# Mixer and routed feed-forward layer on one core: the place of value and gate products in a TensorE step

## The chip, the cores and the metric

One core of one Trainium2 chip runs the whole program. The metric is the device time of one launch in microseconds, the median of the runs shown. TensorE (PE) multiplies matrices and transposes, VectorE (DVE) and ScalarE (ACT) work element by element and empty the PSUM banks that TensorE fills, GpSimd (POOL) does so on SBUF alone, SyncE (SP) issues most DMAs. Each engine works through its own list of instructions in order and meets the others at semaphores.

## The reference

32 batches of 512 tokens with 512 features, all in float32. First a mixing layer with 8 heads of 64, then a feed-forward layer with routing:

```python
q = layernorm(x);  k = v = ctx                     # per batch, 8 heads of 64
ig, fg = concat(q, k, v) @ igate_w.T + b, ... @ fgate_w.T + b
log_D = tril(csum(log_sigmoid(fg)) differences) + ig
D = exp(log_D - rowmax(log_D))
C = (q @ k.T / 8 + einsum('bhvc,vmhc->bhvm', q, rpe[hops])) * D
h = (C / (max(|sum C|, exp(-max)) + 1e-6)) @ v     # then normalised per head, scaled, shifted
x = x + h
y = layernorm(x)
out = x + y @ base_w.T + base_b + 2 * sum over the top-2 experts of weight * (y @ A_e.T) @ B_e.T
```

## The kernel before

**Two stages.** The first gathers rows of `rpe` for every pair of positions and multiplies them with the queries; its products go to DRAM. It is the same before and after. The second stage works in **rounds**, one per batch and two more at the end, and each round has **12 steps**. Five batches are in flight: in a round `rn` is the batch whose inputs are loaded, `rp` the one prepared (contexts and queries transposed, gates), `ra` the one whose attention is computed, `rf` and `rg` the two whose heads are normalised and which go through the feed-forward layer, `rg` being a round further. 28 rounds have all five, three in front and four behind have fewer.

**The order is written out by hand** in the `run` function of each engine, step by step; an instruction waits in its place. The tables say what is due in which step: `C_TURN` 0, 1, 2, 3; `X_TURN` 1, 3, 4, 5; `GATES` 6; `STATS` 10; `BACK` 4, 7, 10; and for the four tiles of the feed-forward layer `TURN` 3, 6, 9, 12, `ROUTE` 4, 7, 10, 13 and `BASE` 5, 8, 11, 14, of which 12, 13, 14 are steps 0, 1, 2 of the next round (tile 3, batch `rg`).

**On TensorE**, in names of the code and lines of the profile:

- `scores(s)`: products of keys and queries with 64 rows, two heads in the two halves of the array (line 1351), and then whole-array transposes that add the stored position products (line 1359). It waits for VectorE's product `mul(s-2)`.
- `weigh(s-1)`, the value product of the step before (line 1375): 128 rows by 64 columns, two heads in two column halves. It waits for `mul(s-1)`. Every third one completes a pair of heads; ScalarE then copies it (`pair_turned`, line 835, into `attT`), TensorE turns it back (`turn_back`) and ScalarE copies and squares it (`pair_out`, lines 844 and 847) for VectorE's sums (`pair_sums`, line 1080).
- `turn_context`, `turn_queries`, `turn_back` and the turn of the feed-forward tile: four whole-array transposes each (all line 1295). Contexts 0 and 1, the queries, the gates, the gate statistics and the base products all use bank 6, so each waits until the one before is copied out.
- the route product (line 1426); `gates` (line 1326), 16 products with 128 rows and 40 columns at partitions 0 and 64; `gate_stats` (line 1336), four transposes of 40 rows.
- `base(r, t)`: the first half of the base product (line 1408), the transpose of `mix` (line 1392, waits for VectorE's line 1161), the second half (1408), and the expert product (line 1410), which waits for ScalarE's copy of the turned `mix` (line 910).

Each product or transpose is followed in its step by what takes it out of PSUM: ScalarE copies contexts (798) and queries (806), gates (899) and the feed-forward tile (914). ScalarE also computes the decays (826) and the roots for the layer norms (748 and 750), VectorE the product of scores and decay `mul(s)` (1072), the query norms (1017), the feed-forward norm (1178), the router chain (1137 to 1161), the output (1123) and the gates (1032 to 1062). On VectorE a step has the order: output, query norm, gates, feed-forward norm, sums, value means, `mul(s)`, query statistics, router, layer norm input.

## Time and profile before

| | us |
|---|---|
| median of 3 runs | 4180.52 (4179.2 to 4185.26) |
| span of the profiled execution | 3689.8 |
| TensorE, VectorE, ScalarE, GpSimd busy in it | 3238.9, 2666.8, 1768.2, 2032.8 |
| stage of the rounds, from about | 1500 to the end |
| one full round | 66.95 |

The span runs from the first to the last instruction; the runs' time also holds what lies around it. A timeline row gives start and duration in us, the engine, the line, the operation with its shape, how many instructions are merged, and in brackets how long the engine idled before and what released it. `PEld` is the load of weights, which overlaps with the products. The duration of merged products is modelled at its end; where one group begins when the other is through is seen by the start of the next.

### The profile page before, as it was taken

To read this page: it belongs to the slowest core of one execution; us is meant where nothing else is said; L and a number is where in the kernel's file an instruction comes from. 1 tells how busy PE (TensorE), PEld (TensorE's weight loads), DVE (VectorE), ACT (ScalarE), POOL (GpSimd) and SP (SyncE) were. 2 spreads that over 40 slices of the span, in tenths; PEclk is the share of its full clock that TensorE was granted. 3 is DMA by queue.
4 is the path that set the end of the run, shared out by engine and by line. 5 is a ranking of instruction groups with operands and counts; after the bars stand their busy time and mean duration, and the time that the engine had idled before them with its cause. 6 is when DMAs were issued, how large, how long until landed. Compare 5 with 4: busy or idle time off the path is not lost.

```text
span 3689.8 us, 70399 instructions
## 1 busy us (share of the span) xinstructions
PE 3238.9 (88%) x24884; PEld 1901.0 (52%) x24884; DVE 2666.8 (72%) x5497; ACT 1768.2 (48%) x4225; POOL 2032.8 (55%) x2248
## 2 busy tenths in 40 slices
PE   5777777777777777699999999999999999999997
PEld 4455555554444444355555555555555555555554
DVE  5554555555555554588988889889888898898885
ACT  2444444444444444455555555555555555555552
POOL 5777777777777776144444444444444444444443
PEclk8888888889898989799999999999999999999999
DMA  8999999999999998555555555555555555555541
GB/s 259 317 317 315 320 317 316 317 323 327 330 320 323 333 324 288 186 157 169 160 154 171 156 170 158 157 170 160 156 172 154 169 156 158 169 162 157 169 142 50
DMA packets 409681, 814.16 MB, mean 221 GB/s; under 512 B 100315, under 2 KB 204763, under 8 KB 407285
## 3 DMA queue, kind: packets, MB, share of 16 engines
q1 hardware_dynamic: 303860, 453.05, 39.9%
q0 software_dynamic: 87040, 285.28, 23.7%
q10 hardware_dynamic: 18432, 71.31, 5.1%
q8 instruction: 203, 3.33, 0.4%
q14 instruction: 146, 1.19, 0.1%
HBM read 632.67 MB, written 176.69 MB: 219 GB/s over the span
## 4 chain that ended last, share of the span: by engine, by line
PE 55%; DMA 15%; POOL 11%; DVE 10%; issue 6%; ACT 2%; SPq 0%; DVEq 0%; ACTq 0%; POOLq 0%
DMA arena<-in_L_xattn_rpe_dram,arena 14%; PE psum L1408 11%; POOL arena L683 8%; PE psum L1351 7%; PE psum L1359 7%; PE psum L1375 7%; PE psum L1268 6%; PE psum L1295 5%; PE psum L1326 3%; PE psum L1410 3%; PE psum L1284 3%; PE psum L1426 3%; POOL arena L674 3%; DVE arena L1178 1%; DVE arena L1072 1%
## 5 line engine op out<-in xcount | busy, mean ns | idle before, releaser
L1268 PE MATMUL psum<-arena 128*128 128x128 f32 x4352 | 695.9, 310 | 243.1 <-DMA arena<-in_L_xattn_rpe_dram,arena 225.2
L683 POOL DMA_INDIRECT arena<-in_L_xattn_rpe_dram,arena x768 | 728.7, 949 | 268.1 <-issue 186.1
L1268 PEld LDWEIGHTS psum<-arena 128*128 128x128 f32 x4352 | 547.2, 158 | 507.0 <-DMA arena<-in_L_xattn_rpe_dram,arena 356.6
L702 POOL TENSOR_SCALAR_AFFINE_SELECT arena<-arena 128x256 f32<-128x256 f32 x256 | 107.2, 419 | 731.3 <-ACT arena L826 628.9
L826 ACT ACTIVATE arena<-arena 128x512 f32<-128x512 f32 (+3 forms) x1024 | 503.0, 559 | 7.3 <-DMA arena<-gate_rows 6.5
L1408 PE MATMUL psum<-arena 128*128 128x512 f32 x1024 | 488.1, 604 | 0.0
L513 DVE COPY arena<-psum 128x512 f32<-128x512 f32 x384 | 263.0, 688 | 280.0 <-PE psum L1268 276.4
L522 DVE COPY arena<-psum 128x416 f32<-128x416 f32 (+15 forms) x512 | 225.1, 441 | 281.3 <-PE psum L1284 278.4
L1072 DVE TENSOR_TENSOR arena<-psum,arena 128x1024 f32<-128x1024 f32 (+1 forms) x384 | 397.5, 1041 | 37.9 <-PE psum L1359 29.0
L1284 PE MATMUL psum<-arena 64*32 64x416 f32 (+7 forms) x8192 | 372.6, 434 | 27.8 <-ACT arena L750 14.9
L674 POOL DMA_INDIRECT arena<-in_L_xattn_rpe_dram,arena x320 | 303.9, 950 | 162.5 <-issue 79.8
L1351 PE MATMUL psum<-arena 64*128 64x512 f32 (+3 forms) x2048 | 381.3, 470 | 0.0
L1359 PE MATMUL psum<-arena 128*128 128x128 f32 x2560 | 364.7, 282 | 0.0
L1375 PE MATMUL psum<-arena 128*64 128x512 f32 (+3 forms) x2048 | 359.2, 450 | 2.4 <-DVE arena L1072 2.3
L522 ACT COPY arena<-psum 128x416 f32<-128x416 f32 (+15 forms) x512 | 199.1, 389 | 331.6 <-PE psum L1284 329.0
L1359 PEld LDWEIGHTS psum<-arena 128*128 128x128 f32 x2560 | 273.6, 141 | 155.5 <-issue 140.1
L513 ACT COPY arena<-psum 128x512 f32<-128x512 f32 x384 | 224.0, 588 | 257.2 <-PE psum L1268 253.7
L1295 PE MATMUL psum<-arena 128*128 128x128 f32 x2048 | 305.4, 282 | 34.4 <-DMA arena<-in_ctx_dram 11.9
L1295 PEld LDWEIGHTS psum<-arena 128*128 128x128 f32 x2048 | 225.3, 142 | 187.5 <-issue 134.6
L1408 PEld LDWEIGHTS psum<-arena 128*128 128x128 f32 x1024 | 177.3, 193 | 160.0 <-issue 152.1
L1351 PEld LDWEIGHTS psum<-arena 64*128 64x128 f32 x2048 | 165.7, 185 | 159.9 <-issue 126.7
L748 ACT ACTIVATE arena<-arena 128x1 f32<-128x1 f32 x384 | 111.3, 290 | 276.5 <-DVE arena L977 149.2
(106 smaller groups left out, 4806.1 us busy)
## 6 DMA issues: line engine op xcount, KB each, us to landing
arena<-in_x_dram SPq DMA_DIRECT2D x256, 256.0 KB, 3.3
arena<-gate_rows SPq DMA_DIRECT2D x128, 512.0 KB, 4.4
arena<-in_x_dram SPq DMA_DIRECT2D x512, 64.0 KB
arena<-in_ctx_dram SPq DMA_DIRECT2D x32, 1024.0 KB, 7.7
out_dram<-arena SPq DMA_DIRECT2D x128, 256.0 KB, 2.3
arena<-in_L_xattn_rpe_dram,arena POOLq DMA_INDIRECT x1088
arena<-hop_products SPq DMA_DIRECT2D x128, 128.0 KB, 2.6
arena<-hop_products SPq DMA_DIRECT2D x128, 120.0 KB, 2.6
```

The costliest lines, as they stand in the source:

```text
L513: copy(rowsT[c % 2][:, o[2], :, o[3] * P:(o[3] + 1) * P], turn_bank(o).rearrange("p (k m) -> p k m", k=KT)).then_inc(*line.inc(o))
L522: copy(hop_out[c][:, lo:lo + width], bank(3 + 2 * (v % 2) + i, width)).then_inc(*line.inc(o))
L683: nc.gpsimd.indirect_dma_start(out=rows[v][:, t, :], out_offset=None, in_=rpe[:, :], in_offset=bass.IndirectOffsetOnAxis(ap=here[:, t, v:v ...
L826: last = nc.scalar.activation(decay[u % 3][:, e, at:at + width], top_pair[p % 2][:, e * S + j * P:e * S + j * P + width], ACT.Exp, bias=st ...
L1072: nc.vector.tensor_tensor(scoresT[u % 2][:, :, 0:width], got[:, :, 0:width], decay[u % 3][:, :, 0:width], ALU.mult).then_inc(dve_a.sem, dv ...
L1268: last = nc.tensor.transpose(turn_bank(o)[:, q * P:(q + 1) * P], own[:, q * P:(q + 1) * P], ident)
L1284: last = nc.tensor.matmul(psum[p * B:(p + 1) * B, at:at + width], qt[half, p, v, :], rowsT[c % 2][half, v, p, 0:width], start=True, stop=True)
L1295: last = nc.tensor.transpose(bank(b)[:, k * P:(k + 1) * P], src[:, k * P:(k + 1) * P], ident)
L1351: nc.tensor.matmul(psum[:, at[e] + col:at[e] + col + width], kT[ra.par][half, p, j * P:(j + 1) * P], qT[ra.par][half, p, j * P:j * P + width],
L1359: last = nc.tensor.matmul(psum[:, at[e] + n * P:at[e] + (n + 1) * P], hop_in[p % 2][:, e, Q_OFF[i] + j * P:Q_OFF[i] + (j + 1) * P], ident, ...
L1375: last = nc.tensor.matmul(psum[e * DH:(e + 1) * DH, 4 * BANK + j * P:4 * BANK + j * P + width], values[ra.par][:, j, HPT * p + e, :], scor ...
L1408: nc.tensor.matmul(bank(6), ffn_xT[t % 2][:, k, :], base_wT[:, k, :], start=(k == 0), stop=False)
```

## The change

Within each step of TensorE's `run`, three calls change their place. `gates` (step 6) and `gate_stats` (step 10) and the value product `weigh(s - 1)` stood between the route product and `turn_back`. They now stand at the end of the step, behind `turn_back`, the turns of context 2 and query tile 0, the turn of the feed-forward tile and the base product. Among the three, `gates` comes ahead of the value product and `gate_stats` behind it. Everything else, semaphores and the other engines' lists included, is as before.

```diff
                         last.then_inc(*pe_f.inc(("route", t)))
-                    if rp and s == GATES:
-                        gates()
-                    if rp and s == STATS:
-                        gate_stats()
-                    if ra and s:
-                        weigh(s - 1)
                     if ra and s in BACK:
                         turn_back(ra, BACK.index(s))
                     if rf and s == 0:
@@
                         turn(7, ffn_x).then_inc(*pe_f.inc(("turn", t)))
                     for t, r in due(BASE, s, rf, rg):
                         base(r, t)
+                    if rp and s == GATES:
+                        gates()
+                    if ra and s:
+                        weigh(s - 1)
+                    if rp and s == STATS:
+                        gate_stats()
                 if ra:
                     weigh(UNITS - 1)
```

The order of the groups on TensorE in the steps where it changes (`scores` first in each; c, xq: turns of a context, a query tile):

| step | before | after |
|---|---|---|
| 1 | c1, route 3, weigh 0, xq0 | c1, route 3, xq0, weigh 0 |
| 2 | weigh 1, c2, base 3 | c2, base 3, weigh 1 |
| 3 | c3, xq1, weigh 2, turn 0 | c3, xq1, turn 0, weigh 2 |
| 4 | xq2, route 0, weigh 3, back 0 | xq2, route 0, back 0, weigh 3 |
| 5 (xq3 ahead of scores) | weigh 4, base 0 | base 0, weigh 4 |
| 6 | gates, weigh 5, turn 1 | turn 1, gates, weigh 5 |
| 7 | route 1, weigh 6, back 1 | route 1, back 1, weigh 6 |
| 8 | weigh 7, base 1 | base 1, weigh 7 |
| 9 | weigh 8, turn 2 | turn 2, weigh 8 |
| 10 | route 2, stats, weigh 9, back 2 | route 2, back 2, weigh 9, stats |
| 11 | weigh 10, base 2, weigh 11 | base 2, weigh 10, weigh 11 |

## Rows read from the trace of the kernel before

**Rows 1.** The page, busy time, its share of the span and instructions of each engine.

```profile
PE 3238.9 (88%) x24884; PEld 1901.0 (52%) x24884; DVE 2666.8 (72%) x5497; ACT 1768.2 (48%) x4225; POOL 2032.8 (55%) x2248
```

**Rows 2.** Windows, 28 full rounds; length, then busy time by engine PE to POOL.

```profile
core 0: us, PE busy (x) PEld busy (x) DVE busy (x) ACT busy (x) POOL busy (x), PEclk, DMA share, GB/s
1667.00:3542.00 1875.00, 1855.52 (x10305) 1027.37 (x10304) 1662.56 (x3473) 998.37 (x2436) 874.73 (x1008) 1.00 0.54 162
```

**Rows 3.** Timeline of PE, gate products (step 6), 29 rounds apart.

```profile
1600.03 3.64 PE L1326 MATMUL psum<-arena 128*40 128x512 f32 x16
...
3542.04 3.64 PE L1326 MATMUL psum<-arena 128*40 128x512 f32 x16
```

**Rows 4.** Timeline of PE, steps 1 and 2 of one round.

```profile
2642.01 0.60 PE L1295 MATMUL psum<-arena 128*128 128x128 f32 x4
2642.45 1.11 PE L1426 MATMUL psum<-arena 128*128 128x138 f32 x8
...
2644.50 0.66 PE L1295 MATMUL psum<-arena 128*128 128x128 f32 x4
2645.09 0.70 PE L1351 MATMUL psum<-arena 64*128 64x256 f32 x4
...
2646.31 1.09 PE L1375 MATMUL psum<-arena 128*64 128x384 f32 x8
2647.32 0.66 PE L1295 MATMUL psum<-arena 128*128 128x128 f32 x4
2647.82 1.88 PE L1408 MATMUL psum<-arena 128*128 128x512 f32 x4
2650.24 0.33 PE L1392 MATMUL psum<-arena 128*128 128x128 f32 x1 [0.54 <-DVE arena L1161]
```

**Rows 5.** Timeline of DVE, end of the router chain of tile 3.

```profile
2649.89 0.29 DVE L1161 TENSOR_TENSOR arena<-psum,arena 128x128 f32<-128x128 f32 x1
```

**Rows 6.** Waits of DVE over 26 rounds: us in total, times, longest.

```profile
DVE arena L1032 <- ACT arena L899: 69.6, 26, 2.7
...
DVE arena L1017 <- ACT arena L750: 26.0, 52, 0.6
DVE arena L1072 <- PE psum L1359: 17.8, 26, 0.7
DVE arena L1080 <- ACT arena L847: 6.5, 26, 0.3
```

**Rows 7.** Timelines of ACT, DVE, PE, steps 3 to 5 of that round.

```profile
2656.73 0.59 ACT L835 COPY arena<-psum 128x512 f32<-128x512 f32 x1
2657.30 0.59 ACT L914 COPY arena<-psum 128x512 f32<-128x512 f32 x1
2657.79 0.91 ACT L826 ACTIVATE arena<-arena 128x256 f32<-128x256 f32 x2
2659.28 0.29 ACT L748 ACTIVATE arena<-arena 128x1 f32<-128x1 f32 x1 [0.58 <-DVE arena L1011]
...
2664.04 0.59 ACT L806 COPY arena<-psum 128x512 f32<-128x512 f32 x1
...
2659.84 0.85 DVE L1017 TENSOR_SCALAR arena<-arena 128x512 f32<-128x512 f32 x1 [0.60 <-ACT arena L750]
...
2657.20 1.14 PE L1351 MATMUL psum<-arena 64*128 64x384 f32 x8
...
2664.94 1.98 PE L1408 MATMUL psum<-arena 128*128 128x512 f32 x4
```

**Rows 8.** Timelines of DVE and PE, steps 11 and 0 ahead of it.

```profile
2632.69 0.29 DVE L1161 TENSOR_TENSOR arena<-psum,arena 128x128 f32<-128x128 f32 x1
2638.93 1.21 DVE L1072 TENSOR_TENSOR arena<-psum,arena 128x1024 f32<-128x1024 f32 x1
...
2633.26 0.27 PE L1392 MATMUL psum<-arena 128*128 128x128 f32 x1
...
2636.62 1.13 PE L1351 MATMUL psum<-arena 64*128 64x512 f32 x4
...
2638.61 1.47 PE L1295 MATMUL psum<-arena 128*128 128x128 f32 x12
```

## The prediction

> **What bounds the kernel now.** The profiled execution spans 3689.8 us; the median of the runs is 4180.52 us. The 490.7 us between them lie outside the span, and the change touches nothing there. Within the span the first 1500 us fill the products with the relative-position table, which the diff does not touch, so only the rounds count. I read the page first (TensorE has most of the busy time [rows 1]), then the windows of the rounds. In the 28 full rounds TensorE is busy 1855.5 of 1875 us, VectorE 1662.6, at a granted clock of 1.00, which is the 2.4 GHz level [rows 2]. From the gate products of one round to those of the next is 66.97 us: (3542.04 - 1600.03) / 29 [rows 3].
>
> A TensorE that is 99% busy looks like the only bound. The timeline says otherwise in one place of every round: in step 2 the base product of tile 3 runs its first half at 2647.82, and the small transpose behind it starts only at 2650.24, having idled 0.54 us for line 1161, VectorE's product that makes `mix` [rows 4]. That product starts at 2649.89 [rows 5], and TensorE starts 0.35 us behind it. Next I read who VectorE itself waits for. Over 26 rounds it waits 69.6 us for the gate copy of step 6 (2.7 a round), 17.8 for `scores(7)` (0.7), 26.0 in 52 waits for ScalarE's query roots (0.5 each) and 6.5 for ScalarE's squares in step 0 (0.25) [rows 6]. So VectorE meets TensorE once a round, at `scores(7)`. From there through step 2 of the next round it works without a wait for TensorE, and its last product there sets when TensorE may go on. The round is a relay: **VectorE from mul(7) to mix(3), then TensorE from mix(3) to scores(7).** Work taken from TensorE in the first part turns into waiting for `mix`; only what is taken or added in the second part counts, and anything that makes VectorE late in the first.
>
> **What the change removes.** Transposes of 4 blocks take 0.44 us between two whole-array groups (2642.01 to 2642.45), 0.50 between a value product and a whole-array group (2647.32 to 2647.82), and 0.59 between a value product and the 64-row score products (2644.50 to 2645.09) [rows 4]. So a change of array tiling costs some 0.06 us on entry and 0.09 on exit, 0.15 together. Before, a step reads 64 rows, whole, 64 columns (value), whole, 64 rows; after it, 64 rows, whole, 64 columns, 64 rows. That is one change fewer in steps 1, 2, 3, 5, 6, 7, 8 and 9, none in 0 and in 4 (turn_queries(3) stands right behind step 4's value product and stays whole-array), two in 10 (the 40-row gate transposes come to stand next to 64-row scores, both row tilings) and two in 11 (value(10) joins value(11)). 12 x 0.15 = **1.8 us less TensorE work a round**. The gate products write 40 columns at partitions 0 and 64, so they are column-tiled like the value product, and stay next to it.
>
> The Trainium skill (TensorEngine Tiling (Array Packing), Key Properties) says that changing the tiling mode drains TensorE; the 0.15 us agree with that rule, and on it alone the change gains the whole 1.8 us a round. The skill also says (TensorE: Matmul & The Clock Gate, What overlaps and what doesn't) that matmuls are strictly first in, first out; the 0.54 us wait agrees, for the ready second half of the base product stands behind it. By that rule a value product that fills such a wait is worth its length there, which speaks against the change.
>
> **What the change adds: three places, summed against the round.**
> 1. Step 2, base(3). Now weigh(1) stands ahead of the base product and fills the time until `mix`; it takes 1.01 us (2646.31 to 2647.32) [rows 4]. Behind the base product it is paid in full after the wait: +1.02 with its rounding, while TensorE only reaches the transpose earlier and idles about 1.9 us instead of 0.54. From there to `scores(7)` steps 3, 5 and 6 lose one change of tiling each, 0.16 to 0.19 measured on these groups: -0.51. Net **+0.51**.
> 2. Step 3 to 5, the copy of attT. weigh(2) now follows the turn of tile 0, and its end moves from 2657.20, where scores(4) starts, by 1.02 - 0.16 = +0.86 to 2658.06. ScalarE takes its instructions in order. Its copy of attT (line 835) began at 2656.73, right behind the copy before it; it now begins near 2658.2. Behind it stand the copy of the normalised tile, a decay, and the roots of query tile 3, which began at 2659.28 and freed VectorE at 2659.84 [rows 7]. Two copies and two decay pieces behind 2658.2 (0.57 + 0.49 + 0.90 by the starts of the group) the roots begin at 2660.2: +0.9, and VectorE, which already waits 0.5 for them, passes it on to the router of tile 0. ScalarE's exponent for that router stands ahead of the copy of query tile 3 out of bank 6, which ended at 2664.04 + 0.59 = 2664.63 [rows 7] and now ends at 2665.5. The base product of tile 0 writes bank 6. It began at 2664.94 with weigh(4) in front of it [rows 7]; it now comes up at 2664.94 + 0.86 - 1.02 - 0.09 = 2664.69 and stands until 2665.55. **+0.86**. The bounds: 0 if ScalarE finds the 0.9 elsewhere, 1.0 at most (the length of weigh(4) that had covered it).
> 3. Step 11 to 0. The product that makes mix(2) starts at 2632.69 and the transpose at 2633.26, 0.57 behind it [rows 8]: 0.22 of slack over the 0.35 of step 2, with weigh(9) and, since, 0.6 of tiling changes ahead. Without weigh(10) ahead too TensorE comes early and waits; the transpose starts 0.22 and, with 0.05 lost behind a wait, the base product ends 0.17 earlier than now and then value(10) and value(11) follow, 0.86 more. scores(0) start at 2636.62 + 0.68. They ended at 2638.61, and mul(0) began at 2638.93 with 0.2 us for the semaphore, so VectorE had 0.12 of slack [rows 8]. mul(0) comes 0.56 later, and the sums of pair 3 behind it, which hang on turn_back(3) and ScalarE's square and already wait 0.25, 0.65 to 0.68 later. This lies in VectorE's part of the relay, and mix(3) moves with it: **+0.68**. The bounds: 0 to 0.86.
>
> Sum: 0.51 + 0.86 + 0.68 = **+2.05 us a round**, 69.0 for 66.97. The pitch holds 29 times, so +59 us. Head and tail (three partial rounds in front, three behind) I take at nothing: their steps have the same edits but longer idle time on either side. Bounds from the rows: -1 us, the changes of tiling in six steps of the tail, to +3 us, two places like the third. Predicted span 3749, predicted time 4180.5 + 59 = **4240 us**.
>
> What else moves, and is covered. turn_queries(0) in step 1 follows the copy of context tile 1 out of bank 6 with only the route product between: the turn ended at 2642.45 and xq0 would start at 2643.5 [rows 4], while such a copy takes 0.6 [rows 7]. gates() in step 6 slips behind the turn of tile 1 by 0.53, but scores(7), 0.7 us the later of the two things VectorE waits for there [rows 6], keep their distance. gate_stats in step 10 ends behind weigh(9), before ScalarE has finished the exponent that its copy stands behind. turn_back(p) comes ahead of weigh(3p+3), a whole step behind the value product that it needs. The turn of tile 2 in step 9 is released by VectorE already, so weigh(8) behind it costs TensorE 0.4 us inside VectorE's part, where there is slack until step 11. No DMA is issued on a moved line; SP's loads of hop products wait for scores, which come later with the round, and the DMA engines are busy 0.54 of the time [rows 2]. The clock stays at 1.00: it held through the present wait in every round [rows 2].
>
> **The rivals.**
> - *Full gain.* TensorE is the bound everywhere, its wait for `mix` is an accident of one place, and VectorE follows the shorter round out of the 4.6 us a round that it waits now [rows 6]. Then 29 x -1.8 = -52: **4128 us**. For it: 99% busy, and VectorE at 89% [rows 2]. It needs VectorE to reach mix(3) at least 1.0 us earlier against TensorE than now; from that point on the first place costs nothing. Against it: the wait recurs in each round with VectorE unbroken before it [rows 4, 6]. It is also what the skill's drain rule alone gives. Chance 0.10.
> - *No measurable change.* The drops outweigh the first place and no other arises: within 8 us of 4180. Chance 0.07.
> - *Step 2 alone.* ScalarE and mul(0) stay covered: +0.51 x 29 = +15, **4195 us**. Chance 0.12.
> - *One of places 2 and 3 is covered:* +1.2 or +1.4 a round, **4215 to 4221 us**. For it: VectorE's instructions stretch and shrink beside GpSimd's, and both rest on margins of 0.1 to 0.3 us. Chance 0.18.
> - *More than three places.* A delayed mask moves GpSimd's products onto VectorE's chain, another us a round: **4270 us**. Chance 0.08.
> - The forecast, 4228 to 4255: 0.45.
>
> **How the numbers follow.** 0.2% is 8 us, about what a measurement of this kernel can tell from no change. Slower holds 0.12 + 0.18 + 0.08 + 0.45 = 0.83, same 0.07, faster 0.10. The range leaves out the full gain, most of "no change" and what lies past one more us a round: 4185 to 4272.
>
> **What the profile after would show.** If I am right: the pitch of the gate products near 69.0; the small transpose of step 2 idle about 1.9 us for line 1161 (0.54 now), and one in step 11 idle as well; a new wait of about 0.9 us ahead of the base product in step 5, for line 806; VectorE's wait for line 750 in step 4 up from 0.6 to about 1.5; mul(0) waiting for scores(0). Four transposes at 0.44 to 0.53 wherever they stood at 0.59 shows the removed changes of tiling, whatever the time does. I am wrong in the first place if VectorE's stretch from mul(7) to mix(3) grows by anything but what place 3 adds; in the second if base(0) starts without idling; and the whole relay falls if the pitch is below 66.9.

## The result and the profile after

The changed kernel is slower, at 4277.82 us (median of 4 runs, 4275.92 to 4280.85) against 4179.94 us (median of 4, 4179.2 to 4185.26) for the kernel before. The ratio is 1.0227, 95% interval [1.0212, 1.0241]. Predicted were 4240 us, range 4185 to 4272. The sign was right, and the cost is 98 us where 59 were forecast.

| us | before | after | after, as predicted |
|---|---|---|---|
| one round (median pitch of the gate products) | 66.95 | 70.17 | 69.0 |
| TensorE busy, a round | 66.2 | 65.0 | 1.8 less |
| TensorE idle, a round | 0.7 | 5.1 | |
| step 2: wait of the small transpose for `mix(3)` | 0.54 | 1.82 | about 1.9 |
| step 5: wait of base(0) for line 806 | none | 1.28 | about 0.9 |
| step 4: VectorE's wait for the roots of query tile 3 | 0.60 | 1.27 | about 1.5 |

3.22 us a round over 29 rounds are 93 of the 98 us; most of the rest lies in the partial rounds at head and tail. (There are four of them at the tail: the prediction counts three.) The two spans, 3689.8 and 4273.9 us, must not be compared. The first stage, which both kernels share, ends near 1500 us in one profile and near 1986 us in the other. Pitches of rounds can be compared.

The windows of after, over some 30 rounds (length; busy time of PE, PEld, DVE, ACT, POOL; granted clock; DMA):

```profile
core 0: us, PE busy (x) PEld busy (x) DVE busy (x) ACT busy (x) POOL busy (x), PEclk, DMA share, GB/s
2000.00:4100.00 2100.00, 1946.31 (x11005) 1087.89 (x11006) 1790.37 (x3662) 1070.02 (x2612) 895.24 (x1072) 1.00 0.52 155
```

Against [rows 2] the clock is unchanged, the full 2.4 GHz. 1946.31 x 70.17 / 2100 = 65.0 us of TensorE work a round. So the change does take work off TensorE, 1.2 us by these records, and the round grows all the same: 5.1 us are idle where 0.7 were. Who it waits for is in the waits of after, 2000 to 3680 us, some 24 rounds (total us, times, longest), PE first and then DVE:

```profile
PE psum L1392 <- DVE arena L1161: 58.0, 69, 2.0
PE psum L1295 <- DVE arena L1178: 29.4, 24, 2.3
PE psum L1408 <- ACT arena L806: 29.3, 23, 1.3
...
DVE arena L1032 <- ACT arena L899: 81.4, 24, 3.4
DVE arena L1017 <- ACT arena L750: 44.5, 51, 2.3
DVE arena L1072 <- PE psum L1359: 32.0, 48, 1.0
```

Before, TensorE had 14.0 us of the first of these over 26 rounds, 0.7 us of the second and none of the third. VectorE, against [rows 6], now waits twice a round for scores (48 times) instead of once. The two places are mul(0) and mul(6), both new. At mul(7) the wait has shrunk from 0.69 to 0.10 us, too short for this table: the gate products come later in step 6, VectorE waits 0.7 us longer for their copy (line 899, 3.4 for 2.7), and mul(7) follows. So TensorE hands over to VectorE at nearly the same point of the round as before, through the gates and through scores(7) at once. The places themselves, in PE's timeline of one round of after:

```profile
2717.39 3.64 PE L1326 MATMUL psum<-arena 128*40 128x512 f32 x16
...
2736.23 0.66 PE L1295 MATMUL psum<-arena 128*128 128x128 f32 x4 [1.18 <-DVE arena L1178]
...
2745.65 0.33 PE L1392 MATMUL psum<-arena 128*128 128x128 f32 x1 [0.51 <-DVE arena L1161]
...
2763.54 0.33 PE L1392 MATMUL psum<-arena 128*128 128x128 f32 x1 [1.82 <-DVE arena L1161]
...
2766.38 1.09 PE L1375 MATMUL psum<-arena 128*64 128x384 f32 x8
...
2779.44 1.96 PE L1408 MATMUL psum<-arena 128*128 128x512 f32 x4 [1.28 <-ACT arena L806]
```

The waits are those of step 9 (1.18), step 11 (0.51), step 2 (1.82, with weigh(1) only after it, at 2766.38) and step 5 (1.28). The answers to [rows 5, 7, 8] in DVE's timeline, from mul(7) of one round to mul(7) of the next:

```profile
2723.59 1.23 DVE L1072 TENSOR_TENSOR arena<-psum,arena 128x1024 f32<-128x1024 f32 x1
...
2725.64 0.67 DVE L1146 TENSOR_SCALAR arena<-arena 128x8 f32<-128x8 f32 x1 [0.26 <-ACT arena L888]
2726.34 1.30 DVE L1149 SCALAR_TENSOR_TENSOR arena<-arena 128x8 f32<-128x8 f32 x1
...
2745.30 0.29 DVE L1161 TENSOR_TENSOR arena<-psum,arena 128x128 f32<-128x128 f32 x1
...
2752.12 1.23 DVE L1072 TENSOR_TENSOR arena<-psum,arena 128x1024 f32<-128x1024 f32 x1 [0.67 <-PE psum L1359]
...
2763.19 0.29 DVE L1161 TENSOR_TENSOR arena<-psum,arena 128x128 f32<-128x128 f32 x1
...
2773.81 1.55 DVE L1017 TENSOR_SCALAR arena<-arena 128x512 f32<-128x512 f32 x1 [1.27 <-ACT arena L750]
2775.28 1.21 DVE L1072 TENSOR_TENSOR arena<-psum,arena 128x1024 f32<-128x1024 f32 x1
...
2793.75 1.23 DVE L1072 TENSOR_TENSOR arena<-psum,arena 128x1024 f32<-128x1024 f32 x1
```

Set against the kernel before, one round of each, taken from the start of mul(7), the lateness builds up in steps (the step named is that of the engine's own list; mix is on VectorE):

| us after mul(7) | before | after | later by |
|---|---|---|---|
| mix(1), step 7 | 4.63 | 5.12 | 0.49 |
| mix(2), step 10 | 21.23 | 21.72 | 0.49 |
| mul(0) | 27.47 | 28.54 | 1.07 |
| mix(3), step 1 | 38.43 | 39.61 | 1.18 |
| mul(4) | 49.15 | 51.70 | 2.55 |
| base(0), on TensorE | 53.48 | 55.85 | 2.37 |
| next mul(7) | 66.95 | 70.17 | 3.22 |

Two of these increments aren't in the prediction. The first 0.49 is a router instruction of line 1149, right behind mul(7), that takes 1.30 us, and 0.70 of the 1.37 between mix(3) and mul(4) is the normalisation of query tile 3 (line 1017), 1.55 us instead of the 0.85 of [rows 7]. Both run on tiles of unchanged size. Beside them GpSimd works on its own tiles. First the neighbours in step 7 and step 4 of after:

```profile
2726.36 1.26 POOL L728 TENSOR_TENSOR arena<-arena 128x512 f32<-128x512 f32 x1
...
2773.81 1.27 POOL L718 TENSOR_TENSOR arena<-arena 128x512 f32<-128x512 f32 x1
```

Then steps 4 and 7 of the kernel before:

```profile
2659.14 1.26 POOL L718 TENSOR_TENSOR arena<-arena 128x512 f32<-128x512 f32 x1
...
2680.58 1.27 POOL L728 TENSOR_TENSOR arena<-arena 128x512 f32<-128x512 f32 x1
...
2680.86 1.02 DVE L1146 TENSOR_SCALAR arena<-arena 128x8 f32<-128x8 f32 x1 [0.27 <-ACT arena L888]
2681.92 0.23 DVE L1149 SCALAR_TENSOR_TENSOR arena<-arena 128x8 f32<-128x8 f32 x1
```

Where one of these VectorE instructions meets one of GpSimd's wide products, it ends when that one ends or just after, however little it has to do: line 1149 at 2727.64 beside GpSimd's 2727.62, line 1146 of before at 2681.88 beside 2681.85, line 1017 at 2775.36 beside 2775.08. Not every VectorE instruction is held; the last section says which. So the price of a meeting follows from what is left of GpSimd's 1.27 us, not from the work of the VectorE instruction. Before, L1146 met 1.0 us of it, and after it L1149 had 0.23. In the changed kernel GpSimd's product starts 0.02 us behind L1149, which pays the whole length, while L1146 in front of it takes 0.67 beside the GpSimd product ahead.

### The profile page after: what moved, and what is told of

The parts are those of the page before. It is cut to its first block, busy times and chain, and to the rows that moved or that the text cites. A ratio compares the mean times of both kernels' runs of the same rounds, so it can differ in the third digit from the quotient of the medians.

```text
span 4273.9 us, 70399 instructions
## 1 busy us (share of the span) xinstructions
PE 3373.2 (79%) x24884; PEld 1948.3 (46%) x24884; DVE 2692.1 (63%) x5497; ACT 1757.1 (41%) x4225; POOL 2005.2 (47%) x2248
## 3 DMA queue, kind: packets, MB, share of 16 engines
q14 instruction: 145, 1.19, 0.1%
## 4 chain that ended last, share of the span: by engine, by line
PE 48%; DVE 28%; issue 9%; another core or an unknown queue 8%; ACT 5%; DMA 2%; DVEq 0%; SPq 0%; POOL 0%; ACTq 0%
PE psum L1268 14%; PE psum L1284 9%; PE psum L1408 5%; DVE arena L1072 5%; PE psum L1375 3%; PE psum L1351 3%; PE psum L1359 3%; PE psum L1326 3%; DVE arena L1149 2%; PE psum L1410 2%; PE psum L1295 2%; DVE arena L522 2%; PE psum L1238 2%; DVE arena L1141 2%
## 5 line engine op out<-in xcount | busy, mean ns | idle before, releaser
L1268 PE MATMUL psum<-arena 128*128 128x128 f32 x4352 | 739.2, 318 | 310.7 <-DVE arena L513 84.9
L1268 PEld LDWEIGHTS psum<-arena 128*128 128x128 f32 x4352 | 564.8, 162 | 610.6 <-issue 450.9
L1284 PE MATMUL psum<-arena 64*32 64x416 f32 (+7 forms) x8192 | 477.7, 464 | 280.2 <-DVE arena L510 78.6
L1072 DVE TENSOR_TENSOR arena<-psum,arena 128x1024 f32<-128x1024 f32 (+1 forms) x384 | 397.8, 1042 | 65.6 <-PE psum L1359 52.5
L1359 PE MATMUL psum<-arena 128*128 128x128 f32 x2560 | 365.4, 282 | 0.0
L1295 PE MATMUL psum<-arena 128*128 128x128 f32 x2048 | 296.2, 278 | 66.1 <-DVE arena L1178 43.1
L1359 PEld LDWEIGHTS psum<-arena 128*128 128x128 f32 x2560 | 274.1, 141 | 155.8 <-issue 140.4
L1284 PEld LDWEIGHTS psum<-arena 64*32 64x32 f32 x8192 | 122.2, 118 | 462.7 <-issue 317.7
L1295 PEld LDWEIGHTS psum<-arena 128*128 128x128 f32 x2048 | 234.2, 142 | 106.2 <-DVE arena L1178 53.8
L1408 PEld LDWEIGHTS psum<-arena 128*128 128x128 f32 x1024 | 182.1, 198 | 178.1 <-issue 176.6
```

What stands on the lines that cost most here:

```text
L1072: nc.vector.tensor_tensor(scoresT[u % 2][:, :, 0:width], got[:, :, 0:width], decay[u % 3][:, :, 0:width], ALU.mult).then_inc(dve_a.sem, dv ...
L1268: last = nc.tensor.transpose(turn_bank(o)[:, q * P:(q + 1) * P], own[:, q * P:(q + 1) * P], ident)
L1284: last = nc.tensor.matmul(psum[p * B:(p + 1) * B, at:at + width], qt[half, p, v, :], rowsT[c % 2][half, v, p, 0:width], start=True, stop=True)
L1295: last = nc.tensor.transpose(bank(b)[:, k * P:(k + 1) * P], src[:, k * P:(k + 1) * P], ident)
L1359: last = nc.tensor.matmul(psum[:, at[e] + n * P:at[e] + (n + 1) * P], hop_in[p % 2][:, e, Q_OFF[i] + j * P:Q_OFF[i] + (j + 1) * P], ident, ...
L1408: nc.tensor.matmul(bank(6), ffn_xT[t % 2][:, k, :], base_wT[:, k, :], start=(k == 0), stop=False)
```

## The experiments

Pitches are medians of the gate products' distance, as above. The kernels named `n`, `m` and `e` ran once each. A single run is enough for a pitch here, since nearly all rounds of a run lie within 0.1 us of its median; and mix(3), which steps 2, 3 and 5 come behind, stands at 38.43 us after mul(7) in the kernel before, 38.41 in `e1` and 38.44 in `e2`, which ran on two different chips. "Late" means that the value product stands at the end of its step, as the change has it.

**The relay, first part.** Is VectorE a bound at all, and what is it that makes it one? In `n_before` and `n_after` three of GpSimd's products work on 32 of 512 columns; the remaining 480 columns of x1 + base bias, of the residual's shift and of the normalised weights are left out.

```diff
-  nc.gpsimd.tensor_tensor(x1_b[t % 2], x1[t % 2], base_b_all, ALU.add)
+  nc.gpsimd.tensor_tensor(x1_b[t % 2][:, 0:32], x1[t % 2][:, 0:32], base_b_all[:, 0:32], ALU.add)
   # the same cut to 0:32 in x_res + ln_b_all and in flat * ln_w1
```

> The kernel before with three of GpSimd's four products per feed-forward tile (x plus base bias, x plus ln_b, times ln_w) made on 32 of the 512 columns; the other columns of these products are left out, so the output is not the reference's. It stands beside the same edit of the kernel after. Theory GpSimd (VectorE instructions that overlap with GpSimd's wide products are stretched, and the change moved GpSimd's products onto VectorE's chain): line 1149 and line 1178 in VectorE's part of the round at their short times (0.23 and 0.55 us), so the pitch of the gate products is shorter than 66.95, by 1 to 3 us. Rival (VectorE's durations have nothing to do with GpSimd): durations and pitch as before, 66.95.

> The kernel after with the same three GpSimd products on 32 of 512 columns (the rest left out). The full kernels differ by 3.22 us a round (70.17 to 66.95), where the relay summed to 2.05. Theory GpSimd: the 1.2 us beyond the sum are stretched VectorE instructions (lines 1146 and 1149 in step 7, 1017 in step 4), so this kernel's pitch stands 2.0 +- 0.4 us above that of the kernel before with the same edit. Rival (a wait that the sum missed makes the 1.2 us): 3.2 us above.

Measured: 65.98 us a round for `n_before`, 64.47 for `n_after` (3660.42 and 3621.57 us). `n_before` comes out just short of the 1 to 3 us that were expected. The change **gains** 1.51 us a round here. Both my theory and its rival had it losing. The windows of 1700 us, `n_before`, then `n_after`:

```profile
1700.00:3400.00 1700.00, 1700.00 (x9483) 947.25 (x9481) 1346.46 (x3199) 921.46 (x2242) 449.82 (x928) 1.00 0.54 164
```

```profile
1700.00:3400.00 1700.00, 1695.64 (x9716) 964.26 (x9715) 1380.72 (x3274) 936.20 (x2302) 505.20 (x950) 1.00 0.56 168
```

The same window of the kernel before:

```profile
1700.00:3400.00 1700.00, 1681.96 (x9362) 933.56 (x9361) 1508.01 (x3154) 905.94 (x2213) 795.06 (x915) 1.00 0.54 162
```

VectorE's own list was not touched, and its busy time falls from 1508.01 x 66.95 / 1700 = 59.4 to 52.3 us a round. **By this pair, seven of VectorE's 59 us are time in which GpSimd holds it.** Without them TensorE never idles in `n_before` (1700.00 of 1700). Its work by the windows goes from 65.98 us a round to 1695.64 x 64.47 / 1700 = 64.30, so the change removes 1.68 of the 1.8 us that I had counted, and 1.51 arrive in the round. The full gain is real, but only with VectorE out of the way.

**One place alone, step 2.** Against the kernel before, only weigh(1) is late.

```diff
+        LATE = (2,)
-                    if ra and s:
+                    if ra and s and s not in LATE:
                         weigh(s - 1)
 ...
                         base(r, t)
+                    if ra and s in LATE:
+                        weigh(s - 1)
```

> The kernel before with one edit: in step 2 the value product stands behind the base product. Relay theory: weigh(1) leaves the wait for mix(3) and is paid behind it; one change of tiling fewer ahead of the wait brings nothing: pitch 66.95 + 1.0 = 67.9, idle ahead of the small transpose in step 2 from 0.54 to 1.7 us. Rival (TensorE is the bound everywhere): one change of tiling fewer, 66.8.

Measured: 67.95 us a round, +1.00, and 3719.72 us beside 3688.81 on the same chip. The value is as expected: TensorE waits for `mix(3)`, as this row of the waits says (lines are one further down here), 1.7 us each time.

```profile
PE psum L1393 <- DVE arena L1162: 42.4, 25, 1.8
```

There is a second effect that I hadn't put in. weigh(1) completes no pair, and still the normalisation of query tile 3 is stretched, in the timeline of DVE:

```profile
2670.30 1.54 DVE L1018 TENSOR_SCALAR arena<-arena 128x512 f32<-128x512 f32 x1 [0.93 <-ACT arena L751]
```

It costs nothing here. Behind the transpose TensorE has no wait in this kernel (its list of waits has three more, 0.9 us in all, in VectorE's part), and from the start of mix(3) to the next mul(7) it is busy 29.19 us where it was 28.18. So the 1.00 is the value product's own time, and the stretch runs beside it.

**One place alone, steps 3 and 5.** The same edit with `LATE = (3, 5)`.

> The kernel before with the value product behind everything in steps 3 and 5 alone. Relay theory: in step 3 nothing is late (weigh(2) ends 0.16 earlier than in the kernel before), and the copy of query tile 3 still ends at its old time; the base product of step 5 comes up 1.3 us earlier, stands for that copy until 0.26 before its old start, and weigh(4) is paid behind it: +0.7 a round, pitch 67.6, with an idle of 1.0 us ahead of line 1408. Rival (tiling changes decide): two fewer, 66.65.

Measured: 68.76 us a round, +1.81, missed by 1.2. The wait at base(0) is there, and a second one that nobody had expected (waits of PE); the stretch comes with them (timelines of DVE and POOL):

```profile
PE psum L1408 <- ACT arena L806: 31.8, 25, 1.3
...
PE psum L1295 <- DVE arena L1178: 11.1, 27, 0.4
```

```profile
2677.82 1.54 DVE L1017 TENSOR_SCALAR arena<-arena 128x512 f32<-128x512 f32 x1 [0.89 <-ACT arena L750]
...
2677.82 1.26 POOL L718 TENSOR_TENSOR arena<-arena 128x512 f32<-128x512 f32 x1
```

mul(4) comes 0.99 us later than before, of which 0.30 is the later start of line 1017 and 0.69 its stretch. The other 0.82 arises behind base(0), which starts when VectorE's and ScalarE's chain lets it and now has weigh(4), 1.0 us, behind it instead of in front. Counted on TensorE, from mix(3) to mul(7), the 1.81 are 1.27 us of waiting at base(0), 0.41 at the turn of tile 0 in step 3, which weigh(2) had covered, and 0.1 more busy time. In the changed kernel the 0.41 isn't there: TensorE comes to that turn a value product later.

**One place alone, step 11.** `LATE = (11,)`.

> The kernel before with the value product behind the base product in step 11 alone. Relay theory: TensorE waits for mix(2), pays weigh(10) behind it, scores(0) come 0.68 later, mul(0) waits for them: +0.6 to +0.7, pitch 67.6. Rival (tiling changes decide): two fewer, 66.65.

Measured: 67.66 us a round, +0.71, as expected. mul(0) is 0.60 later and mix(3) 0.71; TensorE waits twice a round instead of once:

```profile
PE psum L1392 <- DVE arena L1161: 34.4, 50, 0.8
```

**One place alone, step 6.** weigh(5) and the gate products are late in step 6, nothing else.

```diff
+        LATE = (6,)
-                    if rp and s == GATES:
-                        gates()
 ...
                         base(r, t)
+                    if rp and s == GATES:
+                        gates()
+                    if ra and s in LATE:
+                        weigh(s - 1)
```

> The kernel before with one edit: in step 6 the turn of the feed-forward tile stands ahead of gate and value products. Relay theory by its sum: one change of tiling fewer in TensorE's part, -0.16, pitch 66.8. Theory GpSimd: the copy of attT waits for the later value product, with it the decay, the mask and GpSimd's products in step 7, which then overlap line 1149 instead of 1146; line 1149 goes from 0.23 to 1.3 us, mix(1) to mix(3) come 0.5 later: pitch 67.2 to 67.4.

Measured: 67.00 us a round, +0.05, between the two. The exchange is complete (timelines of DVE and POOL, lines one further down): L1150 takes 1.30 us where it took 0.23, and L1147 0.67 for 1.02.

```profile
2739.64 0.67 DVE L1147 TENSOR_SCALAR arena<-arena 128x8 f32<-128x8 f32 x1 [0.26 <-ACT arena L889]
2740.35 1.30 DVE L1150 SCALAR_TENSOR_TENSOR arena<-arena 128x8 f32<-128x8 f32 x1
...
2740.37 1.26 POOL L729 TENSOR_TENSOR arena<-arena 128x512 f32<-128x512 f32 x1
```

mix(1) comes 0.32 later and mix(2) and mix(3) 0.2; a tiling change saved in step 6, in TensorE's part, gives most of it back.

**Steps 1, 7, 8, 9, 10: the savings in VectorE's part.** `LATE = (1, 7, 8, 9, 10)` and gate_stats late, six changes of tiling fewer and none of the three places touched.

> The kernel before with value products (and gate statistics in step 10) behind everything in steps 1, 7, 8, 9 and 10 alone, where VectorE sets the pace: six changes of tiling fewer a round. Relay theory: they only lengthen TensorE's waits for line 1161 and 1178: pitch 66.95 +- 0.1. Rival (TensorE's work counts everywhere): 6 x 0.15 less, 66.05.

Measured: 67.21 us a round, +0.26, outside the expected +-0.1 but far from the rival's 66.05. 0.9 us of work less (0.75 by the timelines) brings no gain at all. TensorE's waits show where it goes:

```profile
PE psum L1295 <- DVE arena L1178: 28.6, 27, 1.3
PE psum L1392 <- DVE arena L1161: 17.7, 27, 0.8
```

Before, the first of these was 0.7 us in 26 rounds and the second 14.0. TensorE comes early to the turn of the feed-forward tile in step 9 and stands 1.06 us each time. That is also where the +0.26 comes from: weigh(8) now stands behind this wait and is paid there, as in the three places. The transpose of step 11 starts 0.27 us later after mul(7), VectorE waits 0.15 us for the base product behind it, and mul(0) is 0.27 later. The prediction had this place down as covered ("there is slack until step 11").

**The two meetings with GpSimd cut out.** In `m_before` and `m_after` GpSimd's x_res + ln_b of tile 1 (step 4) and its product with ln_w1 of tile 2 (step 7) work on 32 of 512 columns; the other 480 of these two tiles are left out.

```diff
+        W1, W2 = (512, 32, 512, 512), (512, 512, 32, 512)
-  nc.gpsimd.tensor_tensor(x_res[t % 2], x_res[t % 2], ln_b_all, ALU.add)
+  nc.gpsimd.tensor_tensor(x_res[t % 2][:, 0:W1[t]], x_res[t % 2][:, 0:W1[t]], ln_b_all[:, 0:W1[t]], ALU.add)
-  nc.gpsimd.tensor_tensor(flat, flat, ln_w1, ALU.mult)
+  nc.gpsimd.tensor_tensor(flat[:, 0:W2[t]], flat[:, 0:W2[t]], ln_w1[:, 0:W2[t]], ALU.mult)
```

> The kernel before with two of GpSimd's products on 32 of 512 columns: x plus ln_b of tile 1 (line 718, step 4) and the product with ln_w of tile 2 (line 728, step 7); the other columns are left out, so the output is not the reference's. In the trace of the kernel before they run beside VectorE's lines 1017 (0.85 us there, 0.54 elsewhere) and 1146 (1.02, 0.29 elsewhere). It stands beside the same edit of the kernel after. Theory GpSimd: both back to their short times, pitch 66.95 less 0.3 to 1.0, so 66.0 to 66.6. Rival (the durations do not come from GpSimd): 66.95.

> The kernel after with the same two GpSimd products on 32 of 512 columns (the rest left out). In its trace line 1149 in step 7 takes 1.30 us (0.23 elsewhere), 1146 0.67, and line 1017 in step 4 1.55 us. Theory GpSimd: these go back to 0.23, 0.29 and 0.54, and the kernel stands 2.1 +- 0.4 us above the kernel before with the same edit, as the relay's sum has it (2.05), for 3.22 between the full kernels. Rival (a missed wait makes the 1.2 us that the sum lacks): 3.2 us above.

Measured: `m_before` 66.74 us a round, just above what was expected, `m_after` 67.60 (3689.02 and 3709.92 us). Taking the two products away is worth 0.21 us in the kernel before and **2.57 us** in the changed one. What is left of the change's loss is 0.86 us a round, where the theory had 2.1 +- 0.4 and the rival 3.2: both missed. The wait at base(0) is nearly gone with them:

```profile
PE psum L1408 <- ACT arena L806: 7.1, 25, 0.3
```

so most of that wait was the stretched line 1017 in front of it, which takes 0.55 us here, and not the roots' delay, which is the same (1.27 us of waiting for them). `m_before` can't fall much further, because TensorE idled only 0.7 us a round in the kernel before, and because VectorE, now earlier, waits for TensorE's base products at two new places, 0.75 us in step 6 (tile 0) and 0.30 in step 0 (tile 2):

```profile
DVE arena L1123 <- PE psum L1410: 26.0, 49, 0.8
```

The 0.86 split into +1.05 from mix(3) to mul(7) and -0.19 up to mix(3). Up to mix(3) the pair isn't clean: GpSimd's other products meet other instructions in the two kernels. The feed-forward norm of step 9 (line 1178) takes 1.44 us in `m_before` and 0.84 in `m_after`.

**The change but for one place.** `e7` is the changed kernel with step 6 in the old order, `e8` with steps 3 and 5 in the old order.

```diff
# condensed: e7 against the changed kernel; e8 the same with weigh alone, and with steps 3 and 5
+                    if rp and s == GATES:
+                        gates()
+                    if ra and s == 6:
+                        weigh(s - 1)
                     if ra and s in BACK:
 ...
-                    if rp and s == GATES:
-                        gates()
-                    if ra and s:
+                    if ra and s and s != 6:
                         weigh(s - 1)
```

> The kernel after with step 6 in its old order (gates, value product, turn of tile 1). GpSimd theory: ScalarE's decay and GpSimd's mask in step 7 come at their old time, line 1149 back from 1.30 to 0.23 and 1146 to 1.0, mix(1) 0.5 earlier; against that one change of tiling (0.16) more in TensorE's part: pitch 69.8. Rival (the missing 0.5 lies elsewhere): 70.3.

> The kernel after with steps 3 and 5 in their old order. The wait for ScalarE's copy of query tile 3 ahead of base(0) goes with them (1.28 us a round in the kernel after), since weigh(4) covers it again; weigh(1) behind the base product of step 2 still delays the copy of attT and with it line 1017, which stays stretched (1.54, as in the kernel with step 2 alone). Step 2 alone cost 1.00, so pitch 66.95 + 1.0 + 0.7 (step 11) + 0.5 (step 6) = 69.1. Rival (the delay of step 4 does not hang on the order of step 5): 70.2 or more.

Measured, in a single run each: `e7` 69.82 us a round, 0.35 less than the changed kernel, with line 1149 back at 0.23 us; `e8` 69.01, 1.16 less, as expected. In `e8` no wait for line 806 is left among TensorE's waits, and line 1017 still takes 1.55 us.

**GpSimd's order.** Can meetings be avoided without leaving anything out? x_res + ln_b (line 718) moves to the front of its step in GpSimd's list, ahead of the masks, so that the two products behind it come 1.2 us earlier. `v1_pool` is the kernel before with that, `v2_pool_after` the changed kernel with it.

```diff
+                    for t in at_step(SCALE, s):
+                        if rf:
+                            pool.wait_ge(xr_loaded[t % 2], rf.b * 32 + 16 * (t // 2 + 1))
+                            nc.gpsimd.tensor_tensor(x_res[t % 2], x_res[t % 2], ln_b_all, ALU.add).then_inc(
+                                *pool_f.inc(("x_b", t)))
 ...                                      # and the same three lines taken out behind the masks
```

> The kernel before, GpSimd's product x plus ln_b moved ahead of the mask that it stood behind in steps 1, 4, 7 and 10; nothing is left out. GpSimd then runs it while it waits for ScalarE's decay, and the two products behind the mask start 1.2 us earlier. Theory GpSimd (a VectorE instruction that meets a GpSimd product ends about 0.3 us after it): line 1017 in step 4 back to 0.55, lines 1146 and 1149 short; the relay loses 0.3 in TensorE's part and 0.5 to 1.5 in VectorE's, where TensorE's base product of step 8 soon binds: pitch 66.2 to 66.7. Rival (no such effect): 66.95.

> The kernel after with the same move of GpSimd's product; nothing is left out. If GpSimd's products cost the kernel after 2.6 us a round (as the narrow ones showed: 70.17 to 67.60), the move gives most of it back: pitch 67.5 to 68.2. Rival (the stretches only move to other instructions): 69.5 or more.

Measured: `v1_pool` 66.43 us a round, 4167.1 beside 4184.13 us, ratio 0.9954 [0.9936, 0.9972]. `v2_pool_after` 67.15 us a round, a little better than expected, 4188.74 us, ratio 1.0006 [0.9995, 1.0017]. **Moving one GpSimd instruction takes 3.02 of the 3.22 us out of the changed kernel**, and 0.5 out of the old one. With GpSimd's order the same on both sides, the change still costs 0.72 us a round.

The pitches came out as expected, but not by the meeting that I had aimed at. Line 1017 in step 4 was to go back to 0.55 us. It takes 1.42 in `v1_pool` (0.86 before) and 1.32 in `v2_pool_after`, since GpSimd's next product now meets it there (`v2_pool_after`, DVE and POOL, lines two further down):

```profile
2756.20 1.32 DVE L1019 TENSOR_SCALAR arena<-arena 128x512 f32<-128x512 f32 x1 [1.26 <-ACT arena L752]
...
2756.20 1.04 POOL L725 TENSOR_TENSOR arena<-arena 128x512 f32<-128x512 f32 x1
```

The gain is made elsewhere. Of the 3.02 us, 2.09 arise up to mix(3): line 1149 behind mul(7) goes from 1.30 to 0.23 us, and line 1099 in step 0, a small instruction that met x_res + ln_b in both kernels, from 1.19 to 0.18. The rest, 0.93, arises behind mix(3), where line 1141 of step 5 goes from 0.84 to 0.14 and the wait at base(0) from 1.28 to 0.36. One meeting that was already there goes too (line 1099), so these 3.02 us are not all cost that the change had brought.

In `v1_pool` TensorE is busy 1790.57 of 1800 us and waits for VectorE nowhere:

```profile
2100.00:3900.00 1800.00, 1790.57 (x9963) 995.15 (x9961) 1574.59 (x3363) 973.26 (x2361) 837.50 (x974) 1.00 0.54 163
```

**Both ideas, put where the relay wants them.** If TensorE's work should fill waits in VectorE's part, and save tiling changes in its own, each value product may have its own best place. `v4_order_pool` puts it in steps 3, 5, 7, 8, 9, 11 ahead of the scores, and in steps 1, 4, 10 at the end; steps 2 and 6 stay; gate_stats moves ahead of the scores of step 11 and the turn of query tile 3 to the end of step 4. GpSimd's order is that of `v1_pool`. `v5_order_pool` is the same with step 7 at the end, `v6_order` is `v5` with GpSimd's list as before.

```diff
+        AHEAD, LATE = (3, 5, 8, 9, 11), (1, 4, 7, 10)      # v4: (3, 5, 7, 8, 9, 11), (1, 4, 10)
+            both = [("score", u)] + ([("value", u - 1)] if u else [])
+            pe_a_steps += both[::-1] if u in AHEAD else both
 ...
+                    if ra and s in AHEAD:
+                        weigh(s - 1)
+                    if rp and s == STATS + 1:
+                        gate_stats()
 ...                                                        # then scores(s), and at the old place:
-                    if ra and s:
+                    if ra and s and s not in AHEAD + LATE:
                         weigh(s - 1)
 ...                                                        # and at the end of the step:
+                    if rp and s == X_TURN[ST - 1] - 1:
+                        turn_queries(ST - 1)
+                    if ra and s in LATE:
+                        weigh(s - 1)
```

> A version by the relay: each value product stands next to another column-tiled or a 64-row group, but never later than now where somebody waits: ahead of the scores of steps 3, 5, 7, 8, 9 and 11, behind everything in 1, 4 and 10, where it was in 2 and 6; query tile 3 is turned in step 4; gate statistics ahead of scores(11); and GpSimd's x plus ln_b ahead of the mask. Relay and GpSimd theories together: 0.6 less in TensorE's part, 0.3 from line 1017, and VectorE's part shorter as in the kernel with the GpSimd move alone, now without its base product of step 8 in the way: pitch 65.0 to 65.8, 1 to 1.6% faster than the kernel before. Rival (tiling changes give nothing here either): as the GpSimd move alone.

Measured: 66.60 us a round, missed; 4176.51 us, ratio 0.998 [0.997, 0.9989]. The timelines show why (lines two further down), PE, then DVE:

```profile
2760.78 1.08 PE L1377 MATMUL psum<-arena 128*64 128x512 f32 x4 [0.37 <-ACT arena L837]
...
2761.44 0.41 DVE L1039 TENSOR_SCALAR arena<-arena 8x512 f32<-8x512 f32 x1
...
2763.98 1.23 DVE L1074 TENSOR_TENSOR arena<-psum,arena 128x1024 f32<-128x1024 f32 x1 [2.13 <-PE psum L1361]
```

weigh(6) stands ahead of scores(7), waits 0.37 us itself and takes 1.0, and VectorE, ready for mul(7), stands 2.13 us. That is the handover of the relay, so a value product ahead of it should be paid in full. `v5` differs in this one place.

> As the version with order and GpSimd move, but the value product of step 7 stands behind turn_back and not ahead of scores(7). In that version VectorE was ready for mul(7) at 64.5 us of the round and waited 2.1 us for scores(7), which had weigh(6) (1.01 us) and its wait for ScalarE's copy (0.37) ahead of them. Relay theory (the round closes at scores(7); what stands ahead of them is paid): 66.60 - 1.4 = 65.2, pitch 65.0 to 65.6, 1.1 to 1.3% faster than the kernel before. Rival (the place of a value product within TensorE's list is worth only its changes of tiling): 66.5.

> The same order of TensorE without the GpSimd move. Relay theory: VectorE's part keeps its 38.4 us to mix(3), TensorE's part loses three to four changes of tiling in steps 3 to 5, 0.45 to 0.6: pitch 66.3 to 66.5. Rival (order alone carries the version): as with the GpSimd move.

Measured: `v5_order_pool` **65.79 us a round, 4144.07 beside 4176.2 us, ratio 0.9922 [0.9908, 0.9937]**, faster than both kernels (by 0.8%) and just above the 65.0 to 65.6 expected. TensorE stands 0.7 us a round for mul(9), the largest wait left:

```profile
PE psum L1377 <- DVE arena L1074: 20.3, 28, 0.9
```

`v6_order` came to 66.86 us a round and a ratio of 0.9995 [0.9982, 1.0008], missed: the order alone brings 0.09 us a round and no time that can be measured. Line 1017 takes 1.30 us in its step 4, and base(0) waits 0.29 for ScalarE. The two moves together bring 1.16 us a round; singly 0.52 and 0.09.

## Why the prediction was right, and where it was wrong

**The relay is right.** The pitch is set by two engines in turn, and work taken off TensorE in VectorE's part turns into waiting: `e5` takes 0.9 us off and gains nothing. The full gain falls: the change gains only where VectorE is 7 us a round shorter, as in `n_before`. The handover near scores(7) is right too: 1.4 us ahead of them in `v4` cost 0.8.

**Where the 1.17 us a round come from that the sum lacks.** The relay gives a clean split at mix(3). I add up TensorE's busy and idle time from there to the next mul(7) in the timelines, medians of 16 rounds:

| us a round | forecast | measured |
|---|---|---|
| up to mix(3), place 3 and nothing else | +0.68 | +1.19 |
| from mix(3): TensorE's busy time (place 1: +1.02 for weigh(1), -0.51 for tiling) | +0.51 | +0.75 |
| from mix(3): wait at base(0) (place 2) | +0.86 | +1.28 |
| sum | +2.05 | +3.22 |

No row is right in size. The first lacks 0.51 us, of which 0.49 are a stretched instruction in step 7; the second gave 0.24 too much to the changes of tiling; the third lacks 0.42, and the stretched line 1017 stands in the chain before it.

**What the change removes.** 12 changes of tiling at 0.15 make 1.8 us. TensorE's busy time by the windows falls by 1.68 in the `n` pair, where TensorE is all but alone the bound, and by 1.2 in the change itself. The Trainium skill's rule (TensorEngine Tiling (Array Packing), Key Properties) that a change of tiling mode drains TensorE agrees in sign; that the cost is a drain, and not another price of changing the form, no run here shows. The gate-row transposes did run among the 64-row scores: in PE's timeline of after they alternate with line 1351 at 2741.89, 2742.04, 2742.09 and 2742.16 us.

**Place 1, step 2: right but for the tiling.** The wait was forecast at 1.9 and is 1.82. `e1` gave the +1.00 that the value product behind the wait costs, and shows it as TensorE's busy time. Of the 0.51 us that fewer changes of tiling were to give back behind it, 0.27 came.

**Place 3, step 11: right.** +0.68 was forecast between mix(2) and mix(3); after shows 1.18 - 0.49 = 0.69 and `e3` 0.71.

**Place 2, steps 3 to 5: this step failed in size.** That ScalarE's late copy would expose base(0) is right. The forecast was +0.86, bounds 0 and 1.0; the wait is 1.28, the place costs 1.16 within the change (`e8`) and 1.81 alone (`e2`), both past the upper bound. The step that failed is "+0.9, and VectorE [...] passes it on to the router of tile 0": it took the 0.85 us of line 1017 as fixed. Before, the line met GpSimd's product at its end, 2659.84 of 2659.14 to 2660.40, and paid 0.3 us over the 0.54 it takes undisturbed. Delayed by ScalarE's roots, and with GpSimd's mask and product delayed by ScalarE's decay, the two start together and it pays the whole 1.27: +0.70. The roots' own delay was no more than forecast: line 1017 starts 0.66 us later after mix(3) than before (forecast 0.9). In `m_after` it does so too, but takes 0.55 us, and the wait at base(0) is 0.3.

**A place that was missing, step 6: put at nothing.** "What else moves, and is covered" had gates() slip by 0.53 with no effect, and looked only at scores(7). The value product behind the gates ends later, and with it ScalarE's copy of attT, the decay, GpSimd's mask and its three products all come 0.59 us later against mul(7). The product with ln_w1 then meets the router instruction of line 1149 from its start, and no longer the one ahead (line 1146): mix(1) +0.49 in after, +0.32 in `e4` alone; without it the change costs 0.35 less (`e7`). That was the rival "more than three places", given 0.08: 4270 us and "another us a round" for delayed masks, measured 4277.8 and 1.17. Its mechanism is what happened, in two places. The 0.45 of the forecast and the range went to a sum with all of VectorE's durations fixed, although one of its rivals names their stretching.

**The parts added up.** Steps 2, 11, 6 and the VectorE part alone cost 1.00 + 0.71 + 0.05 + 0.26 = 2.02 us; `e8`, which has them all, 2.06. Steps 3 and 5 add 1.16 to that, 1.81 if alone, because their wait of 0.41 at the turn of tile 0 is covered once step 2 has its value product late. 2.02 and 1.16 make 3.18 of the 3.22. Forecast 2.05, stretch 0.70 and 0.49 of step 6 would make 3.24, but this near hit is luck: `e1` and `e8` have the whole stretch without paying for it.

**A statement that was wrong without consequence.** The "490.7 us" aren't outside the span. In every run that has both numbers they differ by 1.7 to 2.8 us. The kernel before ran in 3688.81 us on one chip and 3691.82 on another, and in 4176.2 and 4184.13 (medians) on a third; the profile of before is of a run of the first kind, its median of runs of the second.

**What stays open.** Why only 0.27 of the 0.51 us of tiling came behind mix(3), when the `n` pair has nearly the whole 1.8 in the round. How the 1.28 us at base(0) divide between the roots' delay and the stretch when both are there; the 0.3 of `m_after` is for a line 1017 that is shorter than before, too. `v5` lies 0.2 to 0.8 above what was expected of it. No version that leaves nothing out avoids the meeting at line 1017 itself, and most of VectorE's 7 us of meetings were left as they are.

## What to carry to other kernels

Before moving work on the busiest engine, find the closed path that sets the period, across engines: work saved where that engine will wait anyway is worth nothing, and work that used to fill a wait must be paid when it moves behind it. Such a path can be tested place by place, and each part's cost on it read as busy or idle time between the two handovers. A shift of half a microsecond changes which instructions of VectorE and GpSimd meet, and such meetings cost up to a whole GpSimd instruction; look at the ones on the path, and in the trace of a version that moves GpSimd's instructions look again at all of them, since a move that ends one meeting can make another. The best version here changed both orders, and each alone brought less than half.

## What the runs showed of the hardware

- **GpSimd holds some of VectorE's instructions to the end of its own.** VectorE instructions of 0.23, 0.29 and 0.54 us took 1.30, 1.02 and 1.55 beside a GpSimd product of 128x512 float32 on SBUF (1.27 us). Small ones ended 0.01 to 0.05 us behind it, those with 512 columns 0.28 (lines 1017 and 1178) to 0.55 (line 1203, 1.12 us for 0.68). Others aren't held. The products of line 1072, which read PSUM, took 1.20 to 1.23 (128x1024) beside GpSimd and apart from it, and the statistics of line 1009, on an SBUF tile of 128x512, 0.68 either way. GpSimd is held in its turn: its 1.27 us product took 2.17 in `v2_pool_after` beside VectorE's scan (line 1047). The Trainium skill (GPSIMD Engine Reference, Specifications) names an SBUF interface that GpSimd shares with VectorE, in contention for VectorE's instructions with two SBUF inputs or in a 2-port perf mode. The rows agree where they can: line 1149 has two inputs in SBUF and is held, line 1072 has one of its two in PSUM and isn't. Lines 1017 and 1146 have one input tensor and are held; that they run in such a mode no row shows. The price, up to the remaining length of the GpSimd instruction even for a 128x8 tile, comes from these runs.
- **The first stage, which gathers by index, has two lengths:** it ends near 1500 us of the span in all runs on two chips and near 1990 in all runs on a third, with the clock of the rounds the same. Whether the chip makes the difference or something else that changed between the runs, these runs can't tell.
